# Router and sigmoid of a fused attention and expert layer: the router's logits in four f32r passes, the sigmoid by silu in place of the power

## The chip, the core and the metric

The kernel runs on one core of a Trainium2 chip. The metric is the device time of one execution in microseconds (us), as the median of three runs. The core's engines are TensorE (PE in the profile, with its weight loads shown apart as PEld), VectorE (DVE), ScalarE (ACT), GpSimd (POOL) and SyncE (SP, which here issues transfers). Each takes its instructions in program order; semaphores tie them together.

## The reference

The input x has 8 x 2048 = 16384 tokens of 256 features, all in f32. The layer is

```python
x = x + attn(layernorm(x))      # linear attention: Q, K, V of 64; energy = K^T V per batch; out by wo
x = x + ffn(layernorm(x))
# ffn, for each token t:
scores = sigmoid(x @ Wr)                       # Wr: 256 x 8
_, idx = top_k(scores + router_bias, 2)
w = scores[idx] / (sum(scores[idx]) + 1e-9)    # cw: the two weights, zero elsewhere
hid = silu(x @ Wg[e]) * (x @ Wu[e])            # four experts with an MLP of 128
routed = sum_e cw[e] * (hid_e @ Wd[e]) + (cw[4] + cw[6]) * x + cw[7] * relu(x)
out = routed + causal depthwise conv(x, 4 taps) + conv_b
```

The change concerns `scores`: the product with Wr and the sigmoid. Which two experts a token takes depends on the order of the scores, so the logits are needed to nearly full f32.

## The kernel before

The tokens are worked in 32 groups of 512 (four blocks of 128). The body is a software pipeline: in one step, different groups are at different stages (LAG says how many steps behind each stage runs): A transposes and accumulates the Gram matrix for attention, Q projects, B applies attention and takes the second norm's statistics, R transposes x2 and routes, C runs the experts and the convolution, Y writes out. A head runs the first stages of the first groups by hand, then steps 7 to 39 run from `body`. Every fourth step has also the attention's short chain of small matmuls (a chain step: `chain_gramT`, `chain_p1`, `chain_et`, `chain_f`). In the last steps the early stages are empty: steps in which C works, A does not and no chain stands are called drain steps (`drain()`), here steps 34 to 38. Route is still on in steps 7 to 37.

The order on each engine is written out by hand in that engine's `body`. Big products are done in f32r, a matmul type that runs at one pass, with each operand split into a high part and the remainder: `three` issues hi x hi, lo x hi and hi x lo (lines 394 to 396). `gate_up(st, k)` is two such triples with 512 moving columns, `down(st, stage, e)` is twelve matmuls of 256. Plain f32 matmuls show as two records each, with a weight load for each.

What the change touches, in the order of a step:

- PE, `router` (line 512): for each of four token blocks and two halves of the features one f32 matmul, the tokens stationary (128 x 128) and Wr moving (8 columns); its 8 matmuls are 16 records. It stands between `gate_up` 2 and `gate_up` 3. Its result is already in token rows: 128 partitions, 4 x 8 logits.
- ACT, `x2T_out`: copies each transposed half of x2 out of PSUM, once as f32 (`x2T`) and once as f32r (`x2T_hi`); DVE's `x2T_low` makes the remainder `x2T_lo`. `logits_copy` brings the logits out of PSUM.
- POOL, `power`: `enx = (1/e) ** logits` and `den = enx + 1`. It stands between the gate products (`gate_weight`) of experts 1 and 2.
- DVE, `route`: score = 1/den, then bias, top two, weights `cw`: 17 further small instructions, each waiting for the one before by a semaphore. It stands after `hidden` of expert 2 where B is on, and before it where B is off.
- PE, `weights_transpose` (line 575) turns `cw` for four experts; SP stores it and spreads it over all partitions (`cwb`) for the gate products of the next step.

DVE also has the conv's three taps (line 984, two instructions each), the remainders `hid_lo` (line 973) that `down` on PE needs, `residual` (line 1005), which frees the PSUM banks shared by the router, the transposes and attention, and the statistics of both norms.

Of the kernel before, what the change touches and what calls it, by code (L numbers as in the profile page):

```python
# [32 lines left out]
P = 128  # L33
# [6 lines left out]
TAKEN = -2.0e38  # L40

# [66 lines left out]
def program(nc, x, wq, wkT, wvT, woT, wr, rbias, wg, wu, wd, convwb, cw_rows, out):  # L108
# [17 lines left out]
    with ctx:  # L126
# [15 lines left out]
        wr_sb = sb("wr_sb", [P, HC, NE])  # L142
        wgu_hi = sb("wgu_hi", [P, 2, EM, HC, I], F32R)
# [6 lines left out]
        one_e = sb("one_e", [P, TG * NE])  # L150
# [3 lines left out]
        inv_e = sb("inv_e", [P, TG * NE])  # L154
# [29 lines left out]
        x2T_lo = sb("x2T_lo", [P, 2, HC, GT], F32R)  # L184
        logits = sb("logits", [P, TG * NE])
        enx = sb("enx", [P, TG * NE])
        den = sb("den", [P, TG * NE])
# [83 lines left out]
        halo_ready = sem("halo_ready")  # L271
        router_done = sem("router_done")
        logits_ready = sem("logits_ready")
        enx_ready = sem("enx_ready")
        den_ready = sem("den_ready")
# [26 lines left out]
        N_CONST = 8  # L302
        N_LOADS = 6 + 2 * EM + 1
        RT = 7 + 2 * TG
# [86 lines left out]
        def _(pe):  # L391
# [74 lines left out]
            def xn_transpose(st, c):  # L466
# [10 lines left out]
                elif g == 2:  # L477
                    if c == 0:
                        pe.wait_ge(logits_ready, 1)
                    else:  # L480
                        pe.wait_ge(x2Tlo_ready, HC)
# [59 lines left out]
            def attention(st, h):  # L541
# [10 lines left out]
                else:  # L552
                    pe.wait_ge(logits_ready, st.before("R", 1, 1))
# [52 lines left out]
            def head():  # L606
# [25 lines left out]
                router(r)  # L632
                xn_transpose(at("A", 2, NG), 0)
# [18 lines left out]
            def body(st):  # L652
# [24 lines left out]
                if c_on:  # L677
                    gate_up(st, 3)
                if m_on:
                    chain_f(st)  # L680
# [38 lines left out]
        def _(act):  # L719
# [36 lines left out]
            def split_weights():  # L756
                act.wait_ge(w_loaded, 16 * N_LOADS)
                copy(wgu_hi[:, 0].rearrange("p e c i -> p (e c i)"), wg_st.rearrange("p e c i -> p (e c i)"))\
# [62 lines left out]

            def logits_copy(st):
                act.wait_ge(router_done, st.before("R", 1, 1))
# [566 lines left out]
```

## Time and profile before

| | |
|---|---|
| median of three runs | 904.6 us (903.67 to 906.21) |
| the profiled execution | 902.03 us, its span 900.2 us |
| PE busy | 865.2 us, 96% of the span |
| DVE, ACT, POOL busy | 78%, 67%, 63% |
| mean granted TensorE clock | 0.988 of full speed |
| chain that ended last | PE 86%, DVE 6%, POOL 3% |

The span runs from the first to the last instruction of the profiled execution; 1.8 us of its time lie outside it. Busy time of PE counts overlapping records once and each record includes latency, so the distance between the starts of two following matmuls says what each costs, not the record's length. A step in the middle takes about 26 us.

### The profile page before, as it was taken

How to read it: one execution, taken by the hardware profiler on the slowest of the kernel's cores; microseconds unless marked ns; L12 is line 12 of the kernel's file. 1: busy time of each engine (PE TensorE's matmuls, PEld its weight loads, DVE VectorE, ACT ScalarE, POOL GpSimd, SP SyncE). 2: the span in 40 equal slices, each digit the busy share in tenths (PEclk: the TensorE clock that was granted, in tenths of full speed). 3: DMA queues.
4: the chain of work that ended last, by engine and by line, in shares of the span. 5: the costliest groups of instructions: out<-in, count | busy, mean ns of one | idle time of the engine just before them, and what ended most of it. 6: DMA issues, size and time to landing. Idle time of an engine off the chain costs nothing.

```text
span 900.2 us, 16555 instructions
## 1 busy us (share of the span) xinstructions
PE 865.2 (96%) x5402; PEld 765.8 (85%) x5402; DVE 701.8 (78%) x2030; ACT 600.7 (67%) x1212; POOL 565.3 (63%) x654
## 2 busy tenths in 40 slices
PE   5789999999999999999999999999999999999997
PEld 4668889898899988989889888998888898788876
DVE  5757878888778887788787887788878877777675
ACT  5675776777686677668567767666766765665553
POOL 3336776667676657667666767666666765566663
PEclk9989999999999999999999999999999999999999
DMA  9111434432434452343444243545324344344332
GB/s 285 56 53 42 138 121 141 135 104 84 127 118 141 143 138 72 101 136 118 142 141 112 76 120 118 142 141 142 109 66 132 95 117 118 95 117 110 103 90 74
DMA packets 79444, 103.84 MB, mean 115 GB/s; under 512 B 6528, under 2 KB 58880, under 8 KB 79360
## 3 DMA queue, kind: packets, MB, share of 16 engines
q1 hardware_dynamic: 74752, 86.02, 30.0%
q0 software_dynamic: 4608, 16.78, 9.9%
q8 instruction: 43, 0.70, 0.3%
q14 instruction: 41, 0.34, 0.1%
HBM read 68.96 MB, written 17.04 MB: 96 GB/s over the span
## 4 chain that ended last, share of the span: by engine, by line
PE 86%; DVE 6%; POOL 3%; ACT 2%; issue 2%; DMA 0%; POOLq 0%; DVEq 0%; ACTq 0%
PE ps_gu L394 12%; PE ps_gu L396 12%; PE ps_gu L395 12%; PE ps_y L394 6%; PE ps_gram L460 6%; PE ps_y L396 6%; PE ps_y L395 6%; PE ps_sh L512 6%; PE ps_sh L485 3%; PE ps_gram L462 3%; PE ps_sh L502 3%; PE ps_y L444 3%; PE ps_gu L535 2%; PE ps_gu L537 2%; PE ps_sh L561 2%
## 5 line engine op out<-in xcount | busy, mean ns | idle before, releaser
L1273 POOL TENSOR_TENSOR gate<-gate,cwb 128x512 f32<-128x512 f32 x128 | 166.2, 1298 | 135.3 <-ACT gate L728 128.0
L394 PE MATMUL ps_gu<-x2T_hi,wgu_hi 128*128 128x512 f32 x512 | 211.2, 413 | 0.1
L396 PE MATMUL ps_gu<-x2T_hi,wgu_lo 128*128 128x512 f32 x512 | 202.6, 396 | 0.0
L395 PE MATMUL ps_gu<-x2T_lo,wgu_hi 128*128 128x512 f32 x512 | 201.9, 394 | 0.0
L1314 POOL TENSOR_TENSOR enx<-inv_e,logits 128x32 f32<-128x32 f32 x32 | 177.7, 5552 | 9.0 <-ACT logits L721 9.0
L394 PE MATMUL ps_y<-wd_hi,hid_hi 128*128 128x256 f32 x512 | 153.3, 299 | 4.0 <-DVE hid_lo L973 3.1
L396 PE MATMUL ps_y<-wd_hi,hid_lo 128*128 128x256 f32 x512 | 145.5, 284 | 0.0
L395 PE MATMUL ps_y<-wd_lo,hid_hi 128*128 128x256 f32 x512 | 145.1, 283 | 0.0
L984 DVE SCALAR_TENSOR_TENSOR conv<-x2T,conv_w,conv 128x512 f32<-128x512 f32 x192 | 141.2, 773 | 0.0
L966 DVE TENSOR_TENSOR hid<-ps_gu,gate 128x512 f32<-128x512 f32 x128 | 86.0, 672 | 64.6 <-POOL gate L1273 59.0
L728 ACT ACTIVATE gate<-ps_gu 128x512 f32<-128x512 f32 x128 | 75.7, 592 | 65.3 <-PE ps_gu L396 65.2
L396 PEld LDWEIGHTS ps_gu<-x2T_hi,wgu_lo 128*128 128x128 f32 x512 | 96.8, 189 | 22.4
L394 PEld LDWEIGHTS ps_gu<-x2T_hi,wgu_hi 128*128 128x128 f32 x512 | 97.5, 190 | 17.0 <-issue 2.3
L395 PEld LDWEIGHTS ps_gu<-x2T_lo,wgu_hi 128*128 128x128 f32 x512 | 97.3, 190 | 13.9
L394 PEld LDWEIGHTS ps_y<-wd_hi,hid_hi 128*128 128x128 f32 x512 | 97.6, 191 | 6.6 <-DVE hid_lo L973 4.2
L973 DVE TENSOR_TENSOR hid_lo<-hid,hid_hi 128x512 fp32r<-128x512 f32 x96 | 68.7, 716 | 41.5 <-ACT hid_hi L721 41.5
L395 PEld LDWEIGHTS ps_y<-wd_lo,hid_hi 128*128 128x128 f32 x512 | 97.8, 191 | 1.6
L721 ACT ACTIVATE hid_hi<-hid 128x512 fp32r<-128x512 f32 x128 | 80.1, 626 | 27.2 <-DVE hid L966 26.6
L396 PEld LDWEIGHTS ps_y<-wd_hi,hid_lo 128*128 128x128 f32 x512 | 97.5, 190 | 0.0
L1252 POOL TENSOR_TENSOR mv<-mv,eps_ln 128x4 f32<-128x4 f32 x64 | 13.5, 211 | 128.7 <-DVE mv L1016 109.1
L460 PE MATMUL ps_gram<-xn 128*128 128x256 f32 x256 | 77.7, 386 | 0.0
L721 ACT ACTIVATE cwT<-ps_sh 16x128 f32<-16x128 f32 x32 | 8.5, 267 | 98.2 <-PE ps_sh L575 98.1
(103 smaller groups left out, 1870.3 us busy)
## 6 DMA issues: line engine op xcount, KB each, us to landing
cwb<-cw_rows SPq DMA_DIRECT2D x128, 256.0 KB, 3.9
xa<-in_x SPq DMA_DIRECT2D x32, 512.0 KB, 7.9
acc<-in_x SPq DMA_DIRECT2D x32, 512.0 KB, 7.1
acc<-x POOLq DMA_DIRECT2D x32, 512.0 KB, 4.6
out<-acc SPq DMA_DIRECT2D x64, 256.0 KB, 2.7
cwb<-in_wg SPq DMA_DIRECT2D x4, 128.0 KB, 4.0
cwb<-in_wu SPq DMA_DIRECT2D x4, 128.0 KB, 3.8
cwb<-in_wd SPq DMA_DIRECT2D x1, 512.0 KB, 4.6
```

The lines of the kernel that those rows point to most:

```text
L394: nc.tensor.matmul(dst, a_hi, b_hi, start=start, stop=False, skip_group_check=True)
L395: nc.tensor.matmul(dst, a_hi, b_lo, start=False, stop=False, skip_group_check=True)
L396: return nc.tensor.matmul(dst, a_lo, b_hi, start=False, stop=stop, skip_group_check=True)
L460: nc.tensor.matmul(ps_gram[:, 0:H], xn[:, q, t, 0:P], xn[:, q, t, :], start=start, stop=stop, skip_group_check=True)
L512: last = nc.tensor.matmul(b[:, t * NE:(t + 1) * NE], x2T[:, q, c, PAD + t * P:PAD + (t + 1) * P], wr_sb[:, c], start=(c == 0), stop=(c == ...
L721: return nc.scalar.activation(dst, src, ACT.Copy, scale=scale)
L728: nc.scalar.activation(gate[:, e % 2], ps_gu[GU_BANK[2 * e]][:, :], ACT.Silu)\
L966: v.tensor_tensor(hid[:, e % 2], ps_gu[GU_BANK[2 * e + 1]][:, :], gate[:, e % 2], ALU.mult)\
L973: v.tensor_tensor(hid_lo[:, k], hid[:, k], hid_hi[:, k].bitcast(F32), ALU.subtract)\
L984: v.scalar_tensor_tensor(conv[:, c], x2T[:, q, c, k:k + GT], conv_w[:, c, k:k + 1], conv[:, c], ALU.mult, ALU.add).then_inc(conv_ready, 1)
L1273: g.tensor_tensor(gate[:, e % 2], gate[:, e % 2], cwb[:, q, e], ALU.mult).then_inc(gatew_ready, 1)
L1314: g.tensor_tensor(enx[:, :], inv_e[:, :], logits[:, :], ALU.pow).then_inc(enx_ready, 1)
```

## The change

The router becomes four f32r matmuls with the weights stationary: `wr2` holds Wr's high part in columns 0 to 7, its remainder in columns 8 to 15 and zeros up to 128, and `x2T_hi` and `x2T_lo` move through it with 512 columns. The result has 16 rows that matter: for each expert the part with the high weights and that with the remainder. ACT copies them to `logitsT`. One gate-up pair later, after `gate_up` 3, `logits_rows` multiplies each 128-token block of `logitsT` (stationary, 16 x 128) with `pair` (16 x 8, two identity matrices one on the other) in f32: that adds the two parts and gives token rows again. ACT then makes two copies, the logits and their size (Abs).

The sigmoid: DVE takes mag = max(size, 2^-100), ACT dip = silu(-mag), DVE minor = dip / mag (which is minus the sigmoid of -mag), signed = (logits > 0) + minor, score = max(-signed, signed). POOL's `power` goes. The route in drain steps stands earlier on DVE, before the `hid_low` of expert 1, and `x2T_low` of the second half comes after one conv instruction where it came after two. `attention` and a first `xn_transpose` wait for two ACT copies where they waited for one.

```diff
             def router(st):
-                pe.wait_ge(x2T_ready, st.before("R", HC, HC))
+                if st.before("R") == 0:
+                    pe.wait_ge(wrlo_out, 1)
+                b, q = ps_sh[0], st.slot("R", 2)
                 pe.wait_ge(x2Tlo_ready, st.before("R", HC, 1))
-                b, q = ps_sh[0], st.slot("R", 2)
+                pe.wait_ge(x2Thi_ready, st.before("R", HC, HC))
+                for c in range(HC):
+                    nc.tensor.matmul(b[:, :], wr2[:, c], x2T_hi[:, q, c], start=(c == 0), stop=False,
+                                     skip_group_check=True)
+                for c in range(HC):
+                    if c == 1:
+                        pe.wait_ge(x2Tlo_ready, st.before("R", HC, HC))
+                    last = nc.tensor.matmul(b[:, :], wr2[:, c], x2T_lo[:, q, c], start=False, stop=(c == HC - 1),
+                                            skip_group_check=True)
+                last.then_inc(router_done, 1)
+
+            def logits_rows(st):
+                pe.wait_ge(logitsT_ready, st.before("R", 1, 1))
...
                 for t in range(TG):
-                    for c in range(HC):
-                        last = nc.tensor.matmul(b[:, t * NE:(t + 1) * NE],
-                                                x2T[:, q, c, PAD + t * P:PAD + (t + 1) * P], wr_sb[:, c],
-                                                start=(c == 0), stop=(c == HC - 1))
-                last.then_inc(router_done, 1)
+                    last = nc.tensor.matmul(ps_sh[0][:, t * NE:(t + 1) * NE], logitsT[:, t * P:(t + 1) * P], pair[:, :],
+                                            start=(t == 0), stop=(t == TG - 1), skip_group_check=True)
+                last.then_inc(rows_done, 1)
...
+            def logitsT_copy(st):
+                act.wait_ge(router_done, st.before("R", 1, 1))
+                copy(logitsT[:, :], ps_sh[0][0:2 * NE, :]).then_inc(logitsT_ready, 1)
+
             def logits_copy(st):
-                act.wait_ge(router_done, st.before("R", 1, 1))
+                act.wait_ge(rows_done, st.before("R", 1, 1))
...
                 copy(logits[:, :], ps_sh[0][:, 0:TG * NE]).then_inc(logits_ready, 1)
+                nc.scalar.activation(size[:, :], ps_sh[0][:, 0:TG * NE], ACT.Abs).then_inc(logits_ready, 1)
+
+            def score_dip(st):
+                act.wait_ge(mag_ready, st.before("R", 1, 1))
...
+                nc.scalar.activation(dip[:, :], mag[:, :], ACT.Silu, scale=-1.0).then_inc(dip_ready, 1)
...
-                dve.wait_ge(den_ready, st.before("R", 1, 1))
-                done(v.reciprocal(flat(score[:, :, :]), den[:, :]))
+                dve.wait_ge(mag_ready, st.before("R", 1, 1))
+                done(v.reciprocal(rmag[:, :], mag[:, :]))
+                dve.wait_ge(dip_ready, st.before("R", 1, 1))
+                after()
+                done(v.tensor_tensor(minor[:, :], dip[:, :], rmag[:, :], ALU.mult))
+                after()
+                done(v.scalar_tensor_tensor(signed[:, :], logits[:, :], 0.0, minor[:, :], ALU.is_gt, ALU.add))
+                after()
+                done(v.scalar_tensor_tensor(flat(score[:, :, :]), signed[:, :], -1.0, signed[:, :], ALU.mult, ALU.max))
```

On PE, an ordinary step between `gate_up` 2 and `gate_up` 4, before (`ps_sh<-wr_sb,x2T` is the router, `ps_gu` are gate-up products):

```order
L396 MATMUL ps_gu<-x2T_hi,wgu_lo 128x512
L512 MATMUL ps_sh<-wr_sb,x2T 128x8 x8
L394 MATMUL ps_gu<-x2T_hi,wgu_hi 128x512
L395 MATMUL ps_gu<-x2T_lo,wgu_hi 128x512
L396 MATMUL ps_gu<-x2T_hi,wgu_lo 128x512
```

and of the change, where `wr` is `wr2` and `ps_sh<-pair,logitsT` is `logits_rows`:

```order
L406 MATMUL ps_gu<-x2T_hi,wgu_lo 128x512
L523 MATMUL ps_sh<-x2T_hi,wr 128x512 x2
L528 MATMUL ps_sh<-x2T_lo,wr 128x512 x2
L404 MATMUL ps_gu<-x2T_hi,wgu_hi 128x512
L405 MATMUL ps_gu<-x2T_lo,wgu_hi 128x512
L406 MATMUL ps_gu<-x2T_hi,wgu_lo 128x512
L404 MATMUL ps_gu<-x2T_hi,wgu_hi 128x512
L405 MATMUL ps_gu<-x2T_lo,wgu_hi 128x512
L406 MATMUL ps_gu<-x2T_hi,wgu_lo 128x512
L537 MATMUL ps_sh<-pair,logitsT 128x8 x4
L404 MATMUL ps_gu<-x2T_hi,wgu_hi 128x512
```

Eight f32 matmuls with 128 stationary rows go; four of 512 columns come in their place, and four f32 matmuls with 16 stationary rows stand one gate-up pair later.

On DVE, a drain step from expert 1's product `hid` on, before:

```order
L966 TENSOR_TENSOR hid<-ps_gu,gate 128x512
L973 TENSOR_TENSOR hid_lo<-hid,hid_hi 128x512
L1005 TENSOR_TENSOR acc<-ps_sh,acc 128x512 x2
L1013 BN_STATS stats<-acc 128x6 x4
L957 COPY tick<-ident 1x1
L1016 BN_AGGR mv<-stats 128x2 x4
L966 TENSOR_TENSOR hid<-ps_gu,gate 128x512
L1036 RECIPROCAL score<-den 128x32
L1038 TENSOR_TENSOR biased<-score,bias 128x4x8
```

and of the change:

```order
L1014 TENSOR_TENSOR hid<-ps_gu,gate 128x512
L1090 RECIPROCAL rmag<-mag 128x32
L1093 TENSOR_TENSOR minor<-dip,rmag 128x32
L1095 SCALAR_TENSOR_TENSOR signed<-logits,minor 128x32
L1097 SCALAR_TENSOR_TENSOR score<-signed 128x32
L1099 TENSOR_TENSOR biased<-score,bias 128x4x8
```

The whole route now stands between `hid` of expert 1 and its remainder `hid_lo`; `residual`, the statistics and expert 2's `hid` follow after it, and `hid_lo` of expert 2 follows that `hid` directly.

## Rows read from the trace of the kernel before

**Rows 1.** The page's first part: busy us, share of the span, instructions.

```profile
PE 865.2 (96%) x5402; PEld 765.8 (85%) x5402; DVE 701.8 (78%) x2030; ACT 600.7 (67%) x1212; POOL 565.3 (63%) x654
```

**Rows 2.** Busy time by stretch: length, then PE, PEld, DVE, ACT, POOL, clock, DMA.

```profile
92.00:196.00 104.00, 104.00 (x669) 92.97 (x668) 85.15 (x251) 72.49 (x149) 68.89 (x78) 1.00 0.42 119
...
858.00:880.00 22.00, 20.04 (x115) 17.54 (x115) 16.23 (x40) 9.86 (x20) 14.89 (x12) 0.92 0.33 96
```

**Rows 3.** Timeline of PE at the router of an ordinary step: start, length, instruction.

```profile
467.73 0.39 PE L396 MATMUL ps_gu<-x2T_hi,wgu_lo 128*128 128x512 f32 x1
467.96 1.85 PE L512 MATMUL ps_sh<-wr_sb,x2T 128*128 128x8 f32 x16
469.66 0.47 PE L394 MATMUL ps_gu<-x2T_hi,wgu_hi 128*128 128x512 f32 x1
469.98 0.39 PE L395 MATMUL ps_gu<-x2T_lo,wgu_hi 128*128 128x512 f32 x1
```

**Rows 4.** Timeline of PE at `chain_f`, whose stationary operand has 64 rows.

```profile
444.23 0.40 PE L396 MATMUL ps_gu<-x2T_hi,wgu_lo 128*128 128x512 f32 x1
444.56 0.70 PE L603 MATMUL ps_gram<-woT_sb,et 64*128 64x256 f32 x2
445.18 0.50 PE L394 MATMUL ps_gu<-x2T_hi,wgu_hi 128*128 128x512 f32 x1
445.52 0.40 PE L395 MATMUL ps_gu<-x2T_lo,wgu_hi 128*128 128x512 f32 x1
```

**Rows 5.** Timeline of PE at `chain_et`, 64 stationary columns, before the router.

```profile
440.49 0.40 PE L396 MATMUL ps_gu<-x2T_hi,wgu_lo 128*128 128x512 f32 x1
440.82 0.45 PE L597 MATMUL ps_gram<-wkT_sb,p 128*64 128x64 f32 x4
441.19 1.95 PE L512 MATMUL ps_sh<-wr_sb,x2T 128*128 128x8 f32 x16
```

**Rows 6.** Groups by line and form, PEld and DVE: busy, mean ns | idle before.

```profile
L512 PEld LDWEIGHTS ps_sh<-wr_sb,x2T 128*128 128x128 f32 x512 | 63.1, 196 | 6.3 <-issue 2.2 <-ACT x2T L721 1.8
L603 PEld LDWEIGHTS ps_gram<-woT_sb,et 64*128 64x128 f32 x16 | 2.4, 184 | 3.1 <-issue 2.5 <-ACT et L721 0.6
...
L1038 DVE TENSOR_TENSOR biased<-score,bias 128x32 f32<-128x32 f32 x32 | 6.9, 214 | 1.1
```

**Rows 7.** Timeline of ACT just before the router of rows 3.

```profile
467.26 0.59 ACT L721 ACTIVATE x2T_hi<-ps_sh 128x512 fp32r<-128x512 f32 x1
```

**Rows 8.** Timeline of DVE in a drain step.

```profile
839.01 0.69 DVE L973 TENSOR_TENSOR hid_lo<-hid,hid_hi 128x512 fp32r<-128x512 f32 x1 [1.38 <-ACT hid_hi L721]
839.62 1.28 DVE L1005 TENSOR_TENSOR acc<-ps_sh,acc 128x512 f32<-128x512 f32 x2
...
843.31 0.33 DVE L1036 RECIPROCAL score<-den 128x32 f32<-128x32 f32 x1
...
845.75 1.28 DVE L1054 TENSOR_SCALAR wsum_eps<-wsum 128x4 f32<-128x4 f32 x1
...
847.39 0.69 DVE L973 TENSOR_TENSOR hid_lo<-hid,hid_hi 128x512 fp32r<-128x512 f32 x1
```

**Rows 9.** Timeline of PE in the same drain step.

```profile
847.56 0.28 PE L575 MATMUL ps_sh<-ident,cw 128*16 128x128 f32 x1 [1.34 <-DVE cw L1063]
848.14 0.39 PE L394 MATMUL ps_y<-wd_hi,hid_hi 128*128 128x256 f32 x1 [0.30 <-DVE hid_lo L973]
```

**Rows 10.** The chain that ended last, around the last route.

```profile
859.81 5.44 POOL enx L1314
...
872.49 0.58 PE ps_y L394
```

**Rows 11.** Timelines of PE and ACT in the head.

```profile
42.96 3.55 PE L512 MATMUL ps_sh<-wr_sb,x2T 128*128 128x8 f32 x16 [1.55 <-DVE x2T_lo L1070]
...
46.55 0.20 ACT L721 ACTIVATE logits<-ps_sh 128x32 f32<-128x32 f32 x1 [1.54 <-PE ps_sh L512]
...
63.89 1.28 ACT L728 ACT_TABLE_LOAD   x1
```

More of the change, by code:

```diff
@@ L184, in program @@
         x2T_lo = sb("x2T_lo", [P, 2, HC, GT], F32R)
+        logitsT = sb("logitsT", [2 * NE, GT])
         logits = sb("logits", [P, TG * NE])
-        enx = sb("enx", [P, TG * NE])
-        den = sb("den", [P, TG * NE])
+        size = sb("size", [P, TG * NE])
+        mag = sb("mag", [P, TG * NE])
+        dip = sb("dip", [P, TG * NE])
+        rmag = sb("rmag", [P, TG * NE])
+        minor = sb("minor", [P, TG * NE])
+        signed = sb("signed", [P, TG * NE])
         score = sb("score", [P, TG, NE])
@@ L552, in attention @@
                 else:
-                    pe.wait_ge(logits_ready, st.before("R", 1, 1))
+                    pe.wait_ge(logits_ready, st.before("R", 2, 2))
                 if h == 0:
@@ L632, in head @@
                 router(r)
+                logits_rows(r)
                 xn_transpose(at("A", 2, NG), 0)
@@ L678, in body @@
                     gate_up(st, 3)
+                if r_on:
+                    logits_rows(st)
                 if m_on:
@@ L910, in body @@
                     hid_high(st, 0)
+                if r_on:
+                    logits_copy(st)
                 if c_on:
@@ L974, in hid_low, with conv_tap @@
                     .then_inc(hidlo_ready[k], 1)
-            def conv_tap(st, n):
+            def conv_tap(st, n, parts=range(HC)):
                 q, k = st.slot("C", 2), PAD - 1 - n
-                for c in range(HC):
+                for c in parts:
                     if n == 0:
@@ L1020, in flat, with magnitude @@
                 return t.rearrange("p t e -> p (t e)")
+            def magnitude(st):
+                dve.wait_ge(logits_ready, st.before("R", 2, 2))
+                if st.later("R", 1):
+                    dve.wait_ge(dip_ready, st.before("R"))
+                v.tensor_scalar(mag[:, :], size[:, :], LEAST, None, ALU.max).then_inc(mag_ready, 1)
             def route(st):
@@ L1088, in split_weights @@
                 dve.wait_ge(w_loaded, 16 * N_LOADS)
+                dve.wait_ge(wrhi_out, 1)
+                v.tensor_tensor(wr2[:, :, NE:2 * NE], wr_sb[:, :, :], wr2[:, :, 0:NE].bitcast(F32), ALU.subtract)\
+                    .then_inc(wrlo_out, 1)
+                v.tensor_tensor(pair[:, :], ident[0:2 * NE, 0:NE], ident[0:2 * NE, NE:2 * NE], ALU.add)\
+                    .then_inc(pair_ready, 1)
                 dve.wait_ge(whi_ready, NSPLIT)
@@ L1199, in body @@
                 drain = st.drain()
+                if r_on and (drain or not b_on):
+                    route(st)
                 if c_on:
@@ L1205, in body @@
                     norm2_stats(st)
-                if r_on and c_on and not b_on:
-                    route(st)
                 if c_on:
                     hidden(st, 2)
-                if r_on and c_on and b_on:
+                if r_on and b_on and not drain:
                     route(st)
@@ L1310, in skip_factors @@
                 g.tensor_tensor(skip_scale[:, q], coef_rstd[:, :], ones4[:, :], ALU.add).then_inc(skip_ready, 1)
-            def power(st):
-                pool.wait_ge(logits_ready, st.before("R", 1, 1))
-                g.tensor_tensor(enx[:, :], inv_e[:, :], logits[:, :], ALU.pow).then_inc(enx_ready, 1)
-                pool.wait_ge(enx_ready, st.before("R", 1, 1))
-                if st.later("R", 1):
-                    pool.wait_ge(rt, st.before("R", RT, 1 - RT))
-                g.tensor_tensor(den[:, :], enx[:, :], one_e[:, :], ALU.add).then_inc(den_ready, 1)
             def head():
@@ L1324, in head @@
                 norm2_factors(at("B", 1, NG))
-                power(at("R", 0, NG))
                 skip_factors(at("R", 0, NG))
@@ L1332, in body @@
                     gate_weight(st, 1)
-                if r_on:
-                    power(st)
                 if c_on:
```

45 lines of the change are left out of this document (33 added, 12 removed).

## The prediction

> **What bounds the kernel now.** I read the page's busy shares first: PE is busy 96% of the span and no other engine over 78% [rows 1]. A share is only an average, so I then cut the span into stretches. From 92 us on PE is busy in 104.00 of 104.00 us at clock 1.00 [rows 2]; five more stretches of that length up to 716 us read the same to 0.06 us. So for some 25 of the 31 body steps in which the router runs, the time is what PE's own instructions cost, and what ACT, DVE and POOL do is hidden as long as it is not late. POOL's power, over 5 us in each step, is the most visible thing that the change removes, yet in these steps it stands on no path to PE. Third I read the chain of waits at the end: there POOL's power does stand on the path once, for 5.44 us [rows 10], and in the drain steps PE waits for DVE [rows 9]. So the sum has four terms: PE's cost per step, the three drain steps with attention, the last route, and the head.
>
> **PE per step: what goes.** The router's first matmul starts at 467.96 and the second matmul after it at 469.98. A 512-column f32r matmul costs 0.23 (467.73 to 467.96), so the router holds PE for 469.98 - 0.23 - 467.96 = 1.79 us [rows 3]. Its matmuls move only 8 columns, so what is paid is 16 weight loads and the one behind them, that of the next gate-up: 17 x 0.105.
>
> **PE per step: what comes.** The four f32r passes move 512 columns like a gate-up matmul: 4 x 0.23 = 0.92 us, their loads hidden under the matmul before.
>
> `logits_rows` has four f32 matmuls, thus eight records with a load of 128 columns each. The trace has none with 16 stationary rows; the nearest is `chain_f` with 64. The load of 64 rows lasts 184 ns against 196 for 128 rows [rows 6], so fewer rows make it no cheaper; I take 0.105 a load: 8 x 0.105 = 0.84. But entering and leaving a part of the array costs. Before `chain_f`, the last gate-up starts at 444.23 and would free PE at 444.46; `chain_f` starts at 444.56, so 0.10 goes at entry. From 444.46 to the next gate-up's real work (445.52 - 0.23 = 445.29) it is 0.83 us, of which its two records of 256 columns move for 0.43 and 0.21 are two loads that nothing hides (its first and the next gate-up's); so 0.10 at entry and 0.09 at exit are left [rows 4]. `chain_et`, with few moving columns as here, again starts 0.10 late (440.72 to 440.82), and of the 0.37 to the router its four loads of 64 columns take 0.21: 0.16 at exit [rows 5]. I take its 0.16, since its matmuls are as short as ours. So `logits_rows` costs 0.10 + 0.84 + 0.16 + 0.11 (the exposed load of the next gate-up) = 1.21 us. The bounds: with no price for entry and exit 0.95; with an unhidden drain behind each of the four matmuls, 3 x 0.16 more, 1.7.
>
> The Trainium skill (TensorEngine Tiling (Array Packing), Key Properties) says that changing the tiling mode, not just the tile, drains the engine. The trace agrees in rows 4 and 5, for 64 rows and 64 columns; for 32 rows, the mode that 16 stationary rows fall into by that page, no run here shows it yet.
>
> Per ordinary step PE gains -1.79 + 0.92 + 1.21 = +0.34 us. In chain steps `logits_rows` is followed directly by `chain_f`, which has paid its entry already, so +0.24. Steps 8 to 33 are 19 ordinary and 7 chain steps: 6.5 + 1.7 = **+8.2 us**.
>
> Does anything arrive late? The router now needs `x2T_hi` of the second half, which ends at 467.85, 0.11 before PE gets there [rows 7, 3]. The last of the four passes needs `x2T_lo` of the second half: 0.67 of DVE behind that, 468.55, against PE at 467.96 + 0.69 = 468.65. Both are covered, by about 0.1 us; I price them at nothing and keep up to 0.3 a step for a rival. `logits_rows` waits for an ACT copy of some 0.5 us and has 1.39 us of gate-up over it. What ACT gains in each step (0.5 for `logitsT`, 0.2 for `size`, 0.2 for `dip`) and DVE (four small instructions of 0.21 [rows 6]) is under a tenth of a 26 us step in engines at 67% and 78%.
>
> **Drain steps 34 to 36.** Here PE waits for DVE: 1.34 for `cw` and 0.30 for `hid_lo` of expert 2 [rows 9]. The route now stands ahead of expert 1's `hid_lo` and needs `dip`, which ACT makes after `hid_hi` of expert 1. Before, that `hid_hi` was there at 839.01 [rows 8]. Add 0.34 for PE's lateness and 0.25 for `dip`: 839.6. From there DVE has three new instructions 0.65; the route without its reciprocal, 847.39 - 843.31 - 0.36 = 3.7, less 1.1 which one instruction spent at 1.28 where its like takes 0.2, since POOL's gate product is elsewhere now, plus 0.3 for meeting another: 2.9; `hid_lo` of expert 1 0.6; residual, statistics and expert 2's `hid` as before, 843.31 - 839.62 = 3.7; and then ACT's `hid_hi` of expert 2, 0.75, which the route used to cover, and `hid_lo` 0.7. That is 9.3, so PE starts `down` at 848.9 instead of 848.14: +0.8 in each of three steps, **+2.4 us**. Bounds: if the early route lets PE run through, its 1.6 us of waiting go and 1.5 us of half clock that follow it, -3 a step; if two meetings with POOL cost 1 us each, +2.5.
>
> **The last route (step 37).** Without the power, 5.44 us on the chain [rows 10], the next limits are `dip` and PE itself: by the same count `hid_lo` of expert 2 is there at about 870.5 but expert 1's `down` comes late and PE reaches the place at 871.3, against 872.49. That is -1.2, and the half clock after the wait (0.92 in that stretch [rows 2]) gets milder, -0.6: **-1.8 us**.
>
> **The head.** PE's router there runs at half clock, 3.55 us [rows 11]. The four passes take 1.7; then an ACT copy and its signals 0.9, `logits_rows` 2.1 at that clock, and two copies where one was, 0.2 more: +1.3 before the next transposes. `dip` brings its table load (1.28, [rows 11]) forward to before the next `xnT_hi`, 0.5 of it uncovered; its old place had cover. Two small splits of Wr on DVE add 0.3, and one later wait gets 0.3 shorter. **+1.8 us**.
>
> **Sum**: 8.2 + 2.4 - 1.8 + 1.8 = +10.6 us on the profiled execution, 902.03, gives 912.6. That execution was 2.6 under the median of 904.6; the same step from the median gives 915.2, and that is the forecast.
>
> **Rivals.** (a) *No price for changing the part of the array.* A tile of 32 rows could be entered while the matmul before it streams. Then +0.08 x 26 = 2.1, drain 1.6, last route -2.0, head 1.5: +3.2, 907.8. For it: the transposition with 16 stationary columns (line 575) shows no such gap. Against it: rows 4 and 5. Chance 0.18.
> (b) *The weights' and remainders' copies come late.* If ACT's `x2T_hi` misses PE by 0.1 and the last pass waits 0.2 more, each of 19 ordinary steps gains 0.3: +5.7 more, 921. For it: margins of 0.1 only. Against: PE's own lateness in the step doesn't change them. Chance 0.15.
> (c) *Faster, by the drain steps.* If the early route and the missing power let PE run through steps 34 to 37 (-3 x 3 and -4), PE's term alone is left: 8.2 + 1.8 - 13 = -3, 901.6; with (a) it is -8, 896. It decides from the point where expert 2's `hid_lo` is ready before PE asks, 1.6 us sooner than before. Against: DVE's count above is longer, not shorter. Chance 0.11.
> (d) *Faster, by cheap loads.* If a load of 16 rows cost a quarter, eight cost 0.2 and the step gains -0.3: -7.5 in all with the rest cancelling, 897. Nothing but rows 6 speaks on it, and against it. Chance 0.06.
>
> **How the numbers follow.** Forecast 0.50, (a) 0.18, (b) 0.15, (c) 0.11, (d) 0.06. A difference under 0.3% (2.7 us) can't be told from none here. Faster by more than that: (d) and most of (c), with a little of the rest, 0.15. Within it: the rest of (c) and a part of (a), 0.11. Slower: 0.74. The range reaches from 901 (most of (c) and (d) left out below) to 925 (the worse half of (b) and the upper bound of `logits_rows` above).
>
> **What would show it.** In the profile after: the distance from the router's first matmul to the gate-up behind it should be 0.92; `logits_rows` should start 0.10 after the gate-up before it is through, and hold PE about 1.2 us up to the real start of the next, with the weight load of that next one not ahead of it. An ordinary step should be 0.3 us longer. `hid` of DVE should no longer wait for POOL's gate product, with nothing gained by it. In drain steps PE should wait about 1 us at expert 1's `down` and over 1.5 us at expert 2's. I am wrong if `logits_rows` costs under 0.9 us, or if the drain steps get shorter.

## The result and the profile after

| | before | changed |
|---|---|---|
| median | 905.12 us (903.67 to 906.21, 4 runs) | 915.24 us (913.0 to 917.31, 4 runs) |
| profiled execution, its span | 902.03, 900.2 us | 913.0, 911.2 us |
| mean granted clock | 0.988 | 0.993 |
| PE busy | 865.2 us | 873.6 us |
| POOL busy | 565 us | 399 us |

The ratio of the medians is 1.0122, 95% interval [1.0097, 1.0147]: the change makes the kernel slower by 1.2%. The forecast was 915.2 us.

The four executions of the changed kernel took 913.00 and 913.64 us at a mean granted clock of 0.993, and 916.83 and 917.31 us at 0.989 and 0.988. The profiled one is the fastest of them and has no half clock (1.2 GHz, the lower of the clock's two levels) behind the head; the profile before has it in step 7, in the third drain step and at the last route. So the two profiles differ in the clock too, and the terms below are read with that in mind.

The row of busy times on the page after answers to [rows 1]:

```profile
PE 873.6 (96%) x5274; PEld 754.3 (83%) x5274; DVE 726.0 (80%) x2160; ACT 622.4 (68%) x1309; POOL 398.8 (44%) x589
```

POOL lost 166 us and PE gained 8. The next view is the busy time by stretch (length of the stretch, then busy us and instructions of PE, PEld, DVE, ACT, POOL, then granted clock, DMA share, GB/s). The first stretch answers to the first of [rows 2]; the other four run from one router start to the next: three drain steps, then the start of the last route.

```profile
94.00:198.00 104.00, 104.00 (x643) 90.74 (x642) 86.94 (x265) 73.44 (x157) 47.17 (x68) 1.00 0.40 116
...
796.90:821.60 24.70, 22.45 (x134) 18.87 (x134) 17.98 (x56) 14.85 (x31) 10.32 (x14) 1.00 0.37 107
821.60:846.20 24.60, 22.36 (x134) 18.82 (x133) 17.92 (x56) 14.85 (x31) 10.33 (x14) 1.00 0.38 108
846.20:870.90 24.70, 22.45 (x134) 18.85 (x134) 17.99 (x56) 14.85 (x31) 10.32 (x14) 1.00 0.30 86
870.90:895.00 24.10, 23.23 (x132) 19.57 (x132) 21.36 (x49) 11.86 (x25) 11.20 (x11) 1.00 0.39 111
```

In the middle PE is still busy for the whole stretch, so the step's length is still PE's own cost. Here is PE through the router and `logits_rows` of an ordinary step; it answers to [rows 3]:

```profile
474.29 0.40 PE L406 MATMUL ps_gu<-x2T_hi,wgu_lo 128*128 128x512 f32 x1
474.56 0.70 PE L523 MATMUL ps_sh<-x2T_hi,wr 128*128 128x512 f32 x2
475.10 0.63 PE L528 MATMUL ps_sh<-x2T_lo,wr 128*128 128x512 f32 x2
475.56 0.39 PE L404 MATMUL ps_gu<-x2T_hi,wgu_hi 128*128 128x512 f32 x1
...
476.71 0.39 PE L406 MATMUL ps_gu<-x2T_hi,wgu_lo 128*128 128x512 f32 x1
477.03 1.05 PE L537 MATMUL ps_sh<-pair,logitsT 16*128 16x8 f32 x8
478.01 0.50 PE L404 MATMUL ps_gu<-x2T_hi,wgu_hi 128*128 128x512 f32 x1
478.36 0.39 PE L405 MATMUL ps_gu<-x2T_lo,wgu_hi 128*128 128x512 f32 x1
```

A matmul of 512 columns costs 0.23 (474.29 to the point where PE is free, 474.52). The router holds PE from 474.52 to 475.56, 1.04 us (the next gate-up's first record starts there, and its second at 475.79, 0.23 later, so no load is left uncovered). `logits_rows` holds it from 476.71 + 0.23 = 476.94 to the real start of the next gate-up, 478.36 - 0.23 = 478.13: 1.19 us. Before, the router alone held it 1.79.

The same place in the rows of the weight loads shows what nothing covers:

```profile
474.52 0.30 PEld L523 LDWEIGHTS ps_sh<-x2T_hi,wr 128*128 128x128 f32 x2 [0.28 <-issue]
474.87 0.51 PEld L528 LDWEIGHTS ps_sh<-x2T_lo,wr 128*128 128x128 f32 x2
...
477.03 0.96 PEld L537 LDWEIGHTS ps_sh<-pair,logitsT 16*128 16x128 f32 x8 [0.36 <-issue]
478.01 0.19 PEld L404 LDWEIGHTS ps_gu<-x2T_hi,wgu_hi 128*128 128x128 f32 x1
```

Within a triple of gate-ups each load starts one matmul early. The router's first load starts only at 474.52, when the matmul before it is through. `x2T_hi` was out at 473.82 + 0.59 = 474.41 by ACT's row, which answers to [rows 7]:

```profile
473.82 0.59 ACT L748 ACTIVATE x2T_hi<-ps_sh 128x512 fp32r<-128x512 f32 x1
```

That is in time for the matmul and too late for its load, whose place was 474.29.

The third view is PE in the drain steps; its waits answer to [rows 9], and DVE's rows to [rows 8]. First PE:

```profile
857.81 0.39 PE L404 MATMUL ps_y<-wd_hi,hid_hi 128*128 128x256 f32 x1 [0.37 <-DVE hid_lo L1021]
862.87 0.38 PE L404 MATMUL ps_y<-wd_hi,hid_hi 128*128 128x256 f32 x1 [1.88 <-DVE hid_lo L1021]
```

and DVE in the same step:

```profile
853.17 0.80 DVE L1093 TENSOR_TENSOR minor<-dip,rmag 128x32 f32<-128x32 f32 x1 [1.01 <-ACT dip L868]
...
862.13 0.69 DVE L1021 TENSOR_TENSOR hid_lo<-hid,hid_hi 128x512 fp32r<-128x512 f32 x1 [0.69 <-ACT hid_hi L748]
```

The wait for `cw` is gone and two waits for `hid_lo` stand in its place. Around the last route (compare [rows 10]) PE waits once, for expert 1's `hid_lo`:

```profile
882.01 0.39 PE L404 MATMUL ps_y<-wd_hi,hid_hi 128*128 128x256 f32 x1 [0.87 <-DVE hid_lo L1021]
```

Last the head, PE first, which answers to [rows 11]:

```profile
42.78 1.19 PE L523 MATMUL ps_sh<-x2T_hi,wr 128*128 128x512 f32 x2 [1.81 <-ACT x2T_hi L748]
...
45.50 1.87 PE L537 MATMUL ps_sh<-pair,logitsT 16*128 16x8 f32 x8 [0.68 <-ACT logitsT L748]
47.84 1.94 PE L495 MATMUL ps_sh<-ident,xn 128*128 128x128 f32 x8 [0.47 <-ACT size L861]
```

and ACT's table load for `dip`, which now comes here:

```profile
47.71 1.28 ACT L868 ACT_TABLE_LOAD   x1
```

**Where the time went.** Distances between router starts cut both spans into the four terms of the prediction and one step that is in none of them, step 7.

| stretch | before | after | difference | predicted |
|---|---|---|---|---|
| start to first router of the body | 68.60 | 70.26 | +1.7 | +1.8 |
| step 7 | 27.47 | 27.16 | -0.3 | none |
| steps 8 to 33 | 689.6 | 699.5 | +9.9 | +8.2 |
| drain steps 34 to 36 | 72.0 | 74.0 | +2.0 | +2.4 |
| last router to the end | 42.6 | 40.3 | -2.3 | -1.8 |
| sum | 900.2 | 911.2 | +11.0 | +10.6 |

Step 7 has a piece of half clock before (mean clock 0.94) and none after; steps 8 to 33 have none in either profile.

### The profile page after: what moved, and what is told of

It reads as the page before. It is cut to its first block, busy times and chain, and to the rows that moved or that the text cites. A ratio compares the mean times of both kernels' runs of the same rounds, so it can differ in the third digit from the quotient of the medians.

```text
span 911.2 us, 16526 instructions
## 1 busy us (share of the span) xinstructions
PE 873.6 (96%) x5274; PEld 754.3 (83%) x5274; DVE 726.0 (80%) x2160; ACT 622.4 (68%) x1309; POOL 398.8 (44%) x589
## 4 chain that ended last, share of the span: by engine, by line
PE 87%; DVE 6%; ACT 3%; issue 1%; DMA 1%; POOL 1%; POOLq 0%; DVEq 0%; ACTq 0%
PE ps_gu L404 13%; PE ps_gu L406 12%; PE ps_gu L405 12%; PE ps_y L404 6%; PE ps_y L406 6%; PE ps_y L405 6%; PE ps_gram L470 5%; PE ps_sh L537 4%; PE ps_sh L512 3%; PE ps_sh L495 3%; PE ps_y L454 3%; PE ps_gram L472 3%; PE ps_sh L523 2%; PE ps_sh L528 2%; PE ps_sh L585 2%; PE ps_gu L559 2%
## 5 line engine op out<-in xcount | busy, mean ns | idle before, releaser
L1344 POOL TENSOR_TENSOR gate<-gate,cwb 128x512 f32<-128x512 f32 x128 | 171.0, 1336 | 303.7 <-ACT gate L755 293.7
L1021 DVE TENSOR_TENSOR hid_lo<-hid,hid_hi 128x512 fp32r<-128x512 f32 x96 | 85.2, 887 | 39.2 <-ACT hid_hi L748 39.0
L1323 POOL TENSOR_TENSOR mv<-mv,eps_ln 128x4 f32<-128x4 f32 x64 | 23.8, 371 | 138.3 <-DVE mv L1064 119.2
L818 ACT ACTIVATE xn<-xa,shift,rstd 128x256 f32<-128x256 f32 x128 | 66.0, 590 | 8.1 <-POOL shift L1328 8.0
L829 ACT ACTIVATE x<-acc,shift,rstd 128x256 f32<-128x256 f32 x128 | 66.3, 594 | 6.7 <-POOL shift L1328 6.5
```

Source lines behind the costliest of these rows:

```text
L818: nc.scalar.activation(xn[:, q, t], xa[:, q, t], ACT.Identity, bias=shift1[:, f, t:t + 1], scale=rstd1[:, f, t:t + 1]).then_inc(xn_ready, 1)
L829: nc.scalar.activation(x2[:, q, t], acc[:, st.slot("B", 4), t], ACT.Identity, bias=shift2[:, q, t:t + 1], scale=rstd2[:, q, t:t + 1]).then ...
L1021: v.tensor_tensor(hid_lo[:, k], hid[:, k], hid_hi[:, k].bitcast(F32), ALU.subtract)\
L1344: g.tensor_tensor(gate[:, e % 2], gate[:, e % 2], cwb[:, q, e], ALU.mult).then_inc(gatew_ready, 1)
```

## The experiments

Each kernel was timed against the kernel before on the same chip. The kernels below come from three sets, each on a chip of its own, where the kernel before had medians of 903.74 us (sigmoid alone, router alone, `x2T_hi` first, whole array), 903.28 (64 rows, route late, and the two by transposition) and 902.53 (the last row and the sigmoid with DVE's old order). Between kernels of different sets, and against the changed kernel, the ratio compares better than the median. "Ordinary step" is the distance between two router starts in the middle of the profile.

| kernel | median us | ratio to before | ordinary step us |
|---|---|---|---|
| before | 902.5 to 905.1 | 1 | 25.82 |
| changed | 915.24 | 1.0122 [1.0097, 1.0147] | 26.29 |
| sigmoid alone | 905.04 | 1.0031 [1.0011, 1.0051] | 25.91 |
| sigmoid alone, DVE's old order | 901.68 | 0.9993 [0.9982, 1.0004] | 25.83 |
| router alone | 959.27 | 1.062 [1.060, 1.064] | 27.3 to 29.6 |
| `x2T_hi` copied first | 916.62 | 1.0146 [1.0128, 1.0165] | 26.31 |
| whole array | 908.14 | 1.0059 [1.0041, 1.0078] | 26.00 |
| 64 rows | 916.76 | 1.0158 [1.0137, 1.018] | 26.30 |
| route late | 917.17 | 1.0162 [1.0143, 1.018] | 26.29 |
| rows by transposition | **899.98** | 0.9977 [0.9963, 0.9991] | 25.88 |
| the same, route late | 909.95 | 1.0084 [1.0066, 1.0102] | 25.90 |
| the same, `hid` earlier | 905.42 | 1.0033 [1.0019, 1.0047] | 25.97 (one of 26.50) |

**The sigmoid alone.** The old router with its f32 matmuls, the new sigmoid, and the change's order on DVE. One pair of lines, that of the head, stands here for the edit against the kernel before (the comments are mine):

```diff
-                power(at("R", 0, NG))          # POOL
+                magnitude(r)                   # DVE; ACT: Abs in logits_copy, score_dip
```

> The old router (8 f32 matmuls, 16 records) with the new sigmoid, its ACT and DVE instructions and the change's order of DVE. Main theory (PE's cost per step is the router's): the ordinary step goes back to 25.8 us, no gap on PE between steps 8 and 33; drain steps as in the changed kernel (+2 to +2.4 in three), last route -2, head +0.5 or less: 905 us, within 2 of before. Rival (the sigmoid's extra ACT and DVE work slows the steps): ordinary steps stay near 26.3, 912 or more.

Measured: 905.04 us (902.37 to 910.02, 12 runs). The router holds PE 1.79 us again and an ordinary step is 25.91, so the step's added length is the router's. The 0.09 above the old step stands at the first matmul of `gate_up` 4, whose weight load waits for the `hid` of expert 0. The last router to the end is 40.2, as in the changed kernel (40.3): the gain of the last route comes with the sigmoid, not with the router. The drain steps are 24.19 to 24.22, between 23.5 and 24.7.

**The same with DVE's old order.** It asks whether the 0.09 is the sigmoid's own.

```diff
-                    conv_tap(st, 1, (0,))
+                    conv_tap(st, 1)
                 if r_on:
                     x2T_low(st, 1)
-                if c_on:
-                    conv_tap(st, 1, (1,))
```

> The sigmoid alone (old router) with the old place of the conv instruction, ahead of the second x2T_low. Theory: the 0.09 us by which its ordinary step was longer (25.91 against 25.82) came from this place in DVE's order, by which expert 0's hid is late for gate_up 4, not from the sigmoid's instructions: step 25.82, 902 to 903. Rival (it is the sigmoid's extra instructions on ACT and DVE): 25.91 again, 905.

Measured: 901.68 us (901.04 to 903.53, 12 runs), steps of 25.83 and 25.84. The 0.09 was the place of one conv instruction. The sigmoid alone gives no difference that can be told: its profile is 2.4 us shorter from the last router on, about 1.3 longer up to the second router of the body and 0.6 in the drain steps.

**The router alone.** The new router with the old power on POOL and the old place of the route; one pair of lines stands for the edit against the changed kernel.

```diff
-                magnitude(r)
+                power(at("R", 0, NG))          # enx = (1/e) ** logits, den = enx + 1
```

> The new router and logits_rows with the old power on POOL and the old order of route. Main theory: the ordinary step is 26.3 as in the changed kernel, 9 to 10 us over steps 8 to 33, head +1.2, and the power now starts some 3 us later in a step, so in drain steps and at the last route everything behind it is later by 1 to 3 us each: 917 to 924. Rival (the sigmoid is what costs): the ordinary step is 25.8 to 25.9 and the time 906 or less.

Measured: 959.27 us (958.19 to 959.88, 4 runs), far outside what either theory gave. The logits are out 3.79 us after the router's start where it was 2.08 before, 1.7 later (over 3 in chain steps), and the power starts later by as much; it is issued ahead of expert 2's gate product. POOL in one step (a bracket is the idle time before, and what ended it):

```profile
215.82 6.39 POOL L1355 TENSOR_TENSOR enx<-inv_e,logits 128x32 f32<-128x32 f32 x1 [1.46 <-ACT logits L745]
...
222.50 1.30 POOL L1314 TENSOR_TENSOR gate<-gate,cwb 128x512 f32<-128x512 f32 x1
```

and DVE, which waits for that product:

```profile
223.83 0.69 DVE L999 TENSOR_TENSOR hid<-ps_gu,gate 128x512 f32<-128x512 f32 x1 [4.87 <-POOL gate L1314]
```

DVE waits for that product 127.8 us in all, where it was 59.0 before; PE is busy 100.4 to 101.2 of 104 us in the middle. The power is 19.5% of the chain that ended last, where before it stood there once. So the two halves of the change aren't a sum: with the late logits, taking the power away is what keeps POOL off the path. Its 166 us bought that, and nothing else in the middle steps. This is for the order that POOL has here: no run puts the power behind expert 2's gate product, where it might be hidden again.

**`x2T_hi` first.** ACT makes the f32r copy ahead of the f32 one, so that the router's first load can go early.

```diff
-                copy(x2T[:, q, c, PAD:PAD + GT], ps_sh[c][:, :]).then_inc(x2T_ready, 1)
                 copy(x2T_hi[:, q, c], ps_sh[c][:, :]).then_inc(x2Thi_ready, 1)
+                copy(x2T[:, q, c, PAD:PAD + GT], ps_sh[c][:, :]).then_inc(x2T_ready, 1)
```

> The changed kernel with ACT's two copies of each transposed half of x2 swapped: x2T_hi first, then x2T (DVE's remainder waits for both). Theory: the first weight load of the router is not prefetched in ordinary steps because the wait for x2T_hi ends after the time at which that load could go; with x2T_hi 0.5 us earlier the load is hidden, the router holds PE for 0.93 instead of 1.05, and the ordinary step is 0.12 shorter: -3 us, 912. Rival (the load of this stationary operand can't be hidden for another reason, as a change of tile or of operand): router stays at 1.05, no change.

Measured: 916.62 us (915.62 to 918.06, 5 runs). The weight loads show why nothing came of it:

```profile
207.15 0.42 PEld L523 LDWEIGHTS ps_sh<-x2T_hi,wr 128*128 128x128 f32 x2
207.61 0.19 PEld L528 LDWEIGHTS ps_sh<-x2T_lo,wr 128*128 128x128 f32 x1
208.12 0.19 PEld L528 LDWEIGHTS ps_sh<-x2T_lo,wr 128*128 128x128 f32 x1 [0.32 <-DVE x2T_lo L1132]
```

The first load goes one matmul early (207.15), as the theory has it, and then the last pass waits 0.32 for the remainder of the second half. The router holds PE 1.09 us instead of 1.04: the next wait took the place of the first.

**The whole array.** `logitsT` and `pair` get 128 partitions, the rest zero, so that `logits_rows` doesn't use a part of the array (`chain_et` and `chain_f` still do).

```diff
-        pair = sb("pair", [2 * NE, NE])
+        pair = sb("pair", [P, NE])
-        logitsT = sb("logitsT", [2 * NE, GT])
+        logitsT = sb("logitsT", [P, GT])
```

> The changed kernel with logitsT and pair of 128 partitions instead of 16 (the rows beyond 16 are zero), so that logits_rows uses the whole array and nothing else changes. Theory (entering and leaving a part of the array costs 0.10 and 0.16): logits_rows goes from 1.19 to 0.94 in an ordinary step, and its first weight load is prefetched; 0.14 less in a chain step: -5 to -6 us, 909.5. Rival (the price is that of eight loads and the waits alone, whatever the number of rows): no change, 915.

Measured: 908.14 us (906.9 to 910.29, 6 runs), by the ratios 5.7 under the changed kernel (7.1 by the medians); the two intervals lie apart. PE at the place:

```profile
206.70 0.39 PE L406 MATMUL ps_gu<-x2T_hi,wgu_lo 128*128 128x512 f32 x1
206.93 0.95 PE L537 MATMUL ps_sh<-pair,logitsT 128*128 128x8 f32 x8
207.74 0.48 PE L404 MATMUL ps_gu<-x2T_hi,wgu_hi 128*128 128x512 f32 x1
208.06 0.39 PE L405 MATMUL ps_gu<-x2T_lo,wgu_hi 128*128 128x512 f32 x1
```

`logits_rows` starts the moment PE is free (206.70 + 0.23), and holds it to 208.06 - 0.23 = 207.83: 0.90 us, which is its eight loads of 0.105 and 0.06. In all 19 ordinary steps it is 0.90 here, and 1.18 or 1.19 in the changed kernel. So the part of the array costs 0.29 us each time it is entered and left.

**64 rows.** The same with 64 partitions: is it the number of idle rows or the switch?

```diff
-        pair = sb("pair", [2 * NE, NE])
+        pair = sb("pair", [64, NE])
-        logitsT = sb("logitsT", [2 * NE, GT])
+        logitsT = sb("logitsT", [64, GT])
```

> The changed kernel with logitsT and pair of 64 partitions (rows beyond 16 zero): a part of the array of 64 rows instead of 32. Theory (what costs is entering and leaving a part of the array, whatever its size): logits_rows stays at 1.19 us, its first load still not prefetched, 915. Rival (cost follows the rows): between 1.19 and the whole array's 0.90, 911.

Measured: 916.76 us (915.46 to 918.26, 4 runs), step 26.30.

```profile
183.16 0.40 PE L406 MATMUL ps_gu<-x2T_hi,wgu_lo 128*128 128x512 f32 x1
183.49 1.05 PE L537 MATMUL ps_sh<-pair,logitsT 64*128 64x8 f32 x8
...
184.82 0.39 PE L405 MATMUL ps_gu<-x2T_lo,wgu_hi 128*128 128x512 f32 x1
```

Again 0.10 at entry, and 184.82 - 0.23 - 183.39 = 1.20 in all. The price is of the switch and not of the number of rows. The Trainium skill (TensorEngine Tiling (Array Packing), Key Properties) says that the engine drains when the tiling mode changes. The changed kernel and this one agree with it in that such a change costs, for 16 and 64 rows, and they give its size; how much of the 0.29 is a drain and how much the first load that isn't fetched ahead, they don't separate.

**The route late.** In the drain steps the route goes back to its old place on DVE.

```diff
-                if r_on and (drain or not b_on):
-                    route(st)
...
+                if r_on and c_on and not b_on:
+                    route(st)
                 if c_on:
                     hidden(st, 2)
```

> The changed kernel with the route of the drain steps back where it stood before (after residual and statistics; with B on, after expert 2's hid). Theory (the early route costs, since hid_lo of both experts and the residual queue behind it): the three drain periods go from 24.7 back to 23.5 to 24.0, the last route loses a little: -2 us, 913. Rival (the early route is what gets rid of the half clock in these steps): one or two of the three periods at 25 again, no gain or a loss, 915 to 917. Steps 8 to 33 as in the changed kernel under both.

Measured: 917.17 us (916.67 to 917.47, 4 runs). The interval of the ratio begins at 1.0143 and that of the changed kernel ends at 1.0147, so it can't be told from the changed kernel; the theory's gain of 2 us did not come. In the profile the drain steps are 26.07, 24.55 and 26.07 against 24.68, 24.65 and 24.67. One with half clock in it and one without:

```profile
798.00:824.40 26.40, 24.19 (x136) 20.35 (x135) 18.29 (x56) 14.94 (x32) 9.77 (x14) 0.94 0.35 101
824.40:849.00 24.60, 22.39 (x135) 18.97 (x134) 18.25 (x56) 14.73 (x31) 9.79 (x14) 1.00 0.37 108
```

and PE's wait in the first:

```profile
814.26 0.28 PE L599 MATMUL ps_sh<-ident,cw 128*16 128x128 f32 x1 [1.91 <-DVE cw L1124]
```

PE waits about as long in all as with the early route (1.91 + 0.30 against 0.37 + 1.88). Without the lower clock the step is 0.1 shorter; with it, 1.4 longer. The early route doesn't keep the half clock away for certain. The kernel with 64 rows has the changed kernel's route and in its third drain step the same waits, 0.36 and 1.88 us, and yet:

```profile
849.70:875.90 26.20, 23.96 (x134) 20.13 (x134) 17.96 (x56) 14.85 (x31) 10.35 (x14) 0.93 0.30 82
```

Over all profiles 2 of 24 drain steps with the early route have half clock in them (the other is the third of `x2T_hi` first, 26.48 us), and 8 of 12 with the late one.

**Rows by transposition.** The two parts of the logits are brought to token rows by four transposes, which are one record and one load each where an f32 matmul is two, and DVE adds them.

```diff
-                    last = nc.tensor.matmul(ps_sh[0][:, t * NE:(t + 1) * NE], logitsT[:, t * P:(t + 1) * P], pair[:, :],
-                                            start=(t == 0), stop=(t == TG - 1), skip_group_check=True)
+                    last = nc.tensor.transpose(ps_sh[0][:, t * P:(t + 1) * P], logitsT[:, t * P:(t + 1) * P],
+                                               ident[:, :])
...
+                v.tensor_tensor(logits[:, :], flat(lhi[:, :, :]), flat(llo[:, :, :]), ALU.add).then_inc(sums, 1)
+                dve.wait_ge(sums, st.before("R", 2, 1))
+                v.scalar_tensor_tensor(size[:, :], logits[:, :], -1.0, logits[:, :], ALU.mult, ALU.max)\
+                    .then_inc(sums, 1)
```

> logits_rows as four transposes with 128 stationary rows (four weight loads instead of eight, whole array) instead of four f32 matmuls; ACT copies the two parts out, DVE adds them and takes the size (two more small instructions). Theory (PE's cost per step is loads times 0.10 plus passes times 0.23): logits_rows costs 0.44, with the router's 1.05 it is 1.49 against 1.79 of the kernel before: an ordinary step of 25.5 to 25.6, -0.45 against the whole-array matmuls of the earlier run, thus 896 to 898, faster than before. Rival (the longer chain of small instructions to the route shows, in every step or in the drain): ordinary step over 25.8, or over 902.

Measured: 899.98 us (898.63 to 904.55, 12 runs), ratio 0.9977 [0.9963, 0.9991]: a little faster than the kernel before, and by the ratios 13 us faster than the changed one.

```profile
204.37 0.39 PE L407 MATMUL ps_gu<-x2T_hi,wgu_lo 128*128 128x512 f32 x1
204.60 0.60 PE L536 MATMUL ps_sh<-ident,logitsT 128*128 128x128 f32 x4
205.30 0.50 PE L405 MATMUL ps_gu<-x2T_hi,wgu_hi 128*128 128x512 f32 x1
205.64 0.40 PE L406 MATMUL ps_gu<-x2T_lo,wgu_hi 128*128 128x512 f32 x1
```

The transposes and what follows take 205.64 - 0.23 - 204.60 = 0.81 us, where 0.44 was expected. `gate_up` 4 needs the bank that expert 0's `hid` reads, and that is on DVE until then:

```profile
204.56 0.68 DVE L1014 TENSOR_TENSOR hid<-ps_gu,gate 128x512 f32<-128x512 f32 x1
```

So the step is 25.88 and not 25.5. PE isn't busy all the time in the middle (103.69 of 104.00 us), and DVE is at 88.8 of 104, from 84.8 before.

**The same, route late.** The edit is that of the late route above.

> The previous kernel with the route of the drain steps at its old place. By the theory of the first run of this set another -2 us: 895. By its rival no gain.

Measured: 909.95 us (909.12 to 911.27, 5 runs), drain steps of 27.45, 27.21 and 27.26 against 24.22, 24.06 and 24.05. In each PE waits 2.7 to 3.1 us for `cw`, in one piece, and the clock is 0.87 or 0.88. The middle one:

```profile
812.40:839.60 27.20, 24.28 (x131) 20.65 (x130) 18.63 (x58) 14.86 (x31) 9.80 (x14) 0.87 0.33 98
```

Here the early route is worth 10 us, intervals far apart.

**The same, `hid` earlier.** One conv instruction on DVE moves behind expert 0's `hid`.

```diff
-                if c_on:
-                    conv_tap(st, 1, (1,))
...
                     hidden(st, 0)
+                    conv_tap(st, 1, (1,))
```

> The rows by transpose (whole array, four loads) with the conv instruction that stood ahead of DVE's outputs and expert 0's hid moved behind that hid. Theory: in the transpose kernel gate_up 4 waited 0.37 us in each ordinary step for that hid, which ended 0.06 before it; hid is 0.67 earlier now, so the transposes hold PE for 0.44, the ordinary step is 25.5 and the time 891 to 893. Rival (the next wait stands right behind): step still 25.8 or more, 898 or more.

Measured: 905.42 us (903.74 to 909.28, 12 runs). The transposes now hold PE the 0.44 us expected, and yet the step is 25.97. Of the 0.37 us won there, about 0.27 goes at once: the conv's transposes wait for DVE's taps instead. The rest and 0.1 more go late in the step, where the load for a transposition of x waits for ACT's `x` (25 times, 5.5 us in all, against 6 and 2.0). DVE at that place, then PE:

```profile
206.94 2.05 DVE L1032 SCALAR_TENSOR_TENSOR conv<-x2T,conv_w,conv 128x512 f32<-128x512 f32 x3
...
209.05 1.09 PE L455 MATMUL ps_y<-ident,conv 128*128 128x128 f32 x8
```

The rival held. DVE is at 92.7 of 104 us in this kernel, at 88.8 in the one before it. The number of DVE's instructions is the same; some take longer. Over twelve steps in the middle `mag` has 8.8 us more, `hid_lo` 6.5, a small copy within `x2T` 4.1, the conv's taps 1.9, and `wsum_eps` 7.6 less. What `mag` meets is POOL's gate product. DVE and POOL at one `mag`:

```profile
209.96 1.16 DVE L1079 TENSOR_SCALAR mag<-size 128x32 f32<-128x32 f32 x1
209.79 1.29 POOL L1346 TENSOR_TENSOR gate<-gate,cwb 128x512 f32<-128x512 f32 x1 [2.97 <-ACT gate L754]
```

Of its 32 `mag`, 20 take over 0.6 us and the shortest 0.18; each of the 20 starts while the gate product runs, and ends 0.04 us after it. In the kernel before this one `mag` is never long, and 19 of 32 `wsum_eps` are, in the same way.

## Why the prediction was right

The direction, the main term and its mechanism were right. That 915.24 stands beside a forecast of 915.2 is luck: the sum was 0.4 short of the difference of the profiles, the base of 904.6 was 0.5 under the median before, and the terms below miss by up to 1.7 in both directions.

**PE per step: right, 0.13 short.** `logits_rows` was forecast at 1.21 us and takes 1.19. The kernel with the whole array shows that 0.29 of it is for entering and leaving a part of it, where the sum had 0.10 + 0.16 = 0.26; without that price it takes 0.90, where the sum had 0.95. Rival (a), no such price, is out. So is (d), cheap loads of 16 rows: the eight records hold PE for 0.98 us with 16 rows (477.03 to 478.01), and for 0.81 with 128 (206.93 to 207.74).

The router was forecast at 0.92 and takes 1.04. The failed step is "their loads hidden under the matmul before": the margin of 0.11 counted was that of the matmul, while its load wants the operand one matmul earlier. With that 0.12 the gain of an ordinary step is -1.79 + 1.04 + 1.19 = +0.44; measured +0.47. The last 0.03 isn't accounted for. Rival (b) came true to this part, 0.12 of its 0.3; its other half, a wait for `x2T_lo`, shows only where the first is removed (`x2T_hi` first). Of four distances between routers one holds `chain_f` behind `logits_rows`, and there the gain is +0.17 where +0.24 was predicted; the others gain +0.48, +0.48 and +0.43. That is 1.56 in four steps against 1.26, and over 26 steps +9.9 against +8.2.

**"No gain from POOL": right for the changed kernel, and incomplete.** DVE's wait for POOL's gate product fell from 59.0 us in all to 4.0, and the steps got no shorter:

```profile
DVE hid L1014 <- POOL gate L1344: 4.0, 3, 1.3
```

The prediction treated the power as something that costs nothing while hidden. With the new, later logits it costs some 45 us by the ratios (router alone, 959.27, against 915.24). That the two edits depend on one another was in no step of the prediction.

**Drain steps: right in sum, by luck: two errors cancel.** The two steps that had full clock before were 23.5 us, and all three after are 24.7: +1.2 each, where +0.8 was predicted. But the third one before, that of [rows 8, 9], ran at clock 0.93 and was 25.01, and in the profile after none does: -1.5, which the sum did not have. 3 x 1.17 - 1.5 = +2.0. That -1.5 belongs to the execution that was profiled: with the same waits the kernel with 64 rows has half clock in the third step (26.2 us). The failed step is the size of DVE's chain and of PE's own lengthening, +0.8 for +1.2. The chain itself was read well: from `dip` to PE's start at expert 2 the prediction counted 9.3 us, the profile has 862.87 - 853.17 = 9.7. The wait at expert 1's `down` was forecast at about 1 us and is 0.37; that at expert 2's, over 1.5, is 1.88. With the sigmoid alone the same steps are 24.2, so about 0.7 of each 1.2 comes with the sigmoid and the route's place, the rest with PE's own lengthening. What the late route would have done was left at a bound in the prediction; it is not better (route late) and with a faster router much worse.

**The last route: right in its direction, its parts not shown one by one.** -2.3 measured, -1.8 predicted. Power gone, PE waits 0.87 there instead of 0.28 + 1.69, -1.1, and the clock of the stretch is 1.00 where it was 0.93, worth about -1.7, where the prediction had -1.2 and -0.6; PE's own work is longer there too. The kernels with the sigmoid alone have 40.2 us from the last router on, as the changed one (40.3): it comes with the sigmoid. But the half clock isn't bound to the power: the router alone has the power, waits of 1.35 and 1.70 us and no half clock in that stretch, and 42.6 us.

**The head: right in the profile, and not to be told better than to some 2.5 us.** +1.7 measured, +1.8 predicted, to the first router of the body; to the second it is +1.35. To the second router the changed kernel has 97.4 us, and the kernels with nearly the same head, 64 rows and route late, have 99.95 and 98.95. Both the part ahead of step 7 (69.7 to 71.8 us) and step 7 itself (27.2 us at clock 1.00, 30.3 at 0.89) differ among the three. The two profiles with the sigmoid alone are 0.5 and 1.3 above the one before, and differ too much to split the term.

## What to carry to other kernels

On the engine that bounds the kernel, count weight loads and changes between parts of the array, not multiplied elements: pad a small operand to the whole array, and prefer a transpose to a small f32 matmul. A long instruction off the critical path is worth nothing where it stands but decides how far its inputs may move; two edits that touch its input and its length must be priced together. When the bound engine is cut by a few tenths of a microsecond, list first what is due within that margin on the others: in two of the cuts here (`x2T_hi` first, `hid` earlier) another wait took all of the gain or more.

## What the runs showed of the hardware

- Entering and leaving a part of the array costs 0.29 us in all for 16 or 64 of 128 rows, with the load that this leaves uncovered; none of it for a matmul on 128 rows. Not every small operand pays it: the transposition of `cw`, with 16 stationary columns, holds PE for 0.11 us (465.64 to 465.75) and starts without a gap. Why, the runs don't show.

```profile
465.64 0.27 PE L599 MATMUL ps_sh<-ident,cw 128*16 128x128 f32 x1
465.75 0.60 PE L495 MATMUL ps_sh<-ident,xn 128*128 128x128 f32 x4
```

- A weight load went ahead where its operand was out when the matmul before it started, and not where it came just after. In every ordinary step of the changed kernel `x2T_hi` was out 0.13 us after that start, in time for its matmul, and the load began only at that matmul's end: 0.12 us of the router's 1.04. With `x2T_hi` copied first it was out 0.36 us ahead, and the load began together with the matmul before. In the idle times of the weight loads after (us in all, times, longest) both costs show as gaps that nothing explains:

```profile
PEld ps_sh L537 <- issue: 11.2, 31, 0.4
PEld ps_sh L523 <- issue: 8.4, 24, 2.0
```

- Half clock after PE's waits in the drain steps: with 1.34 and 0.30 us (the kernel before) in one of three steps, with 1.91 and 0.30 (route late) in two of three, with 2.04 and 0.30 (router alone) in two of three, with 2.7 to 3.1 in one piece in all three (mean clock 0.87 to 0.88). With a first wait of 0.4 to 0.6 and a second of 1.9 to 2.0 us, in eight profiles, it was 2 of 24. A wait of 1.88 us was followed by it in one kernel and not in another, so the length of the waits isn't the whole of it; what decides stays open.
- The power of 128 x 32 elements on POOL took 5.43 us in the median of 32, 5.98 at most, in the kernel before, and 5.85 and 6.40 in the kernel with the router alone.
- A small instruction of DVE that started while POOL's gate product of 128 x 512 ran ended 0.03 to 0.04 us after that product: `mag` took 1.16 us there instead of 0.18.
